# Moving the row normalisations behind the low query half, one value product into slot 4, and half of the probability casts to GpSimd

## What is computed

```
xn = layernorm(ctx, gamma_media, beta_media)
ln = layernorm(layernorm(x), gamma_lat, beta_lat)
q  = ln @ Wq + bq;   k, v = split(concat([xn, ln]) @ Wkv + bkv)
attn = softmax(q k^T * 128**-0.5)            # per head, 256 x 512
x1 = x + concat_heads(attn @ v) @ Wo + bo
```

## Time and profile before

| | |
|---|---|
| median of 3 runs (lowest, highest) | 1898.28 us (1897.49, 1898.93) |
| the profiled execution | 1898.91 us |
| its span | 1896.6 us |
| TensorE busy / VectorE / ScalarE / GpSimd | 95% / 78% / 70% / 21% of the span |

### The profile page before, as it was taken

One profiled execution on the slowest core, in us unless ns is written; L12 is line 12 of the kernel. 1 busy time (PEld: TensorE's weight loads), 2 busy tenths in 40 slices (PEclk: granted clock), 3 DMA queues, 4 the chain that ended last, 5 costly groups with the idle time before them and its releaser, 6 DMA issues.

```text
span 1896.6 us, 39969 instructions
## 1 busy us (share of the span) xinstructions
PE 1804.8 (95%) x12874; PEld 1672.3 (88%) x12874; DVE 1484.5 (78%) x3620; ACT 1330.2 (70%) x2554; POOL 390.1 (21%) x610
## 2 busy tenths in 40 slices
PE   6889999999999999999689999999999999999999
PEld 5778888888888878888578999999999999999998
DVE  6787788788787787777567788888888888888876
ACT  5777787777776777767556777766777777666753
POOL 1222222222222222222244111111111011111100
PEclk9999999999999999999889999999999999999999
DMA  4454565455554444344353933342442323433400
GB/s 143 85 126 106 127 148 123 103 130 138 125 135 82 91 84 93 80 91 79 79 109 111 298 73 73 80 85 57 85 86 64 83 65 74 84 79 63 86 7 12
DMA packets 355420, 182.25 MB, mean 96 GB/s; under 512 B 292512, under 2 KB 340512, under 8 KB 355360
## 3 DMA queue, kind: packets, MB, share of 16 engines
q1 hardware_dynamic: 346656, 146.88, 32.1%
q0 software_dynamic: 8704, 34.61, 10.2%
HBM read 97.29 MB, written 21.23 MB: 62 GB/s over the span
## 4 chain that ended last, share of the span: by engine, by line
PE 80%; DVE 10%; issue 4%; ACT 3%; DMA 1%; POOL 1%; DVEq 0%; SPq 0%; POOLq 0%; ACTq 0%
PE ring L2016 9%; PE ring L2018 9%; PE ring L2017 8%; PE ring L726 8%; PE ring L728 8%; PE ring L727 8%; PE sim L726 3%; PE sim L2018 3%; PE sim L2016 3%; PE sim L2017 3%; PE sim L728 3%; PE sim L727 3%; DVE a_parts L647 2%; PE ps_x L726 2%; PE ps_x L727 2%
## 5 line engine op out<-in xcount | busy, mean ns | idle before, releaser
L2016 PE MATMUL ring<-b_xch,b_wel 128*128 128x256 f32 x1024 | 289.8, 283 | 0.5 <-DVE b_act_e L1639 0.5
L2018 PE MATMUL ring<-b_xcl,b_weh 128*128 128x256 f32 x1024 | 286.4, 280 | 0.0
L2017 PE MATMUL ring<-b_xch,b_weh 128*128 128x256 f32 x1024 | 286.1, 279 | 0.0
L394 POOL TENSOR_SCALAR a_parts<-a_pr,a_rinv 128x512 f16<-128x512 f32 x240 | 170.4, 725 | 413.0 <-DVE a_rinv L638 310.2
L486 ACT ACTIVATE a_pr<-sim,a_nmax 128x512 f32<-128x512 f32 x256 | 173.2, 684 | 40.9 <-DVE a_nmax L627 39.9
L2017 PEld LDWEIGHTS ring<-b_xch,b_weh 128*128 128x128 f32 x1024 | 193.4, 189 | 0.0
L2016 PEld LDWEIGHTS ring<-b_xch,b_wel 128*128 128x128 f32 x1024 | 192.1, 188 | 0.7 <-DVE b_act_e L1639 0.7
L2018 PEld LDWEIGHTS ring<-b_xcl,b_weh 128*128 128x128 f32 x1024 | 192.1, 188 | 0.0
L1355 ACT ACTIVATE b_heh<-b_act_e 128x512 fp32r<-128x512 f32 x128 | 80.7, 630 | 146.7 <-DVE b_act_e L1639 112.8
L627 DVE TENSOR_REDUCE a_nmax<-sim 128x1 f32<-128x512 f32 x256 | 165.8, 682 | 11.3 <-PE sim L728 10.6
L647 DVE SCALAR_TENSOR_TENSOR a_parts<-a_pr,a_rinv,a_parts 128x512 f16<-128x512 f32 x240 | 169.8, 748 | 6.0 <-POOL a_parts L394 6.0
(11 more groups left out here) (362 smaller groups left out, 6350.1 us busy)
## 6 DMA issues: line engine op xcount, KB each, us to landing
b_w2l_raw<-in_W2T POOLq DMA_DIRECT2D x16, 1088.0 KB, 8.7
b_even_b<-rows_between SPq DMA_DIRECT2D x16, 1024.0 KB, 5.6
b_w1l_raw<-in_W1T POOLq DMA_DIRECT2D x16, 1024.0 KB, 8.4
b_w1l_raw<-in_We SPq DMA_DIRECT2D x8, 768.0 KB, 4.6
expert_halves<-b_w1h SPq DMA_DIRECT2D x8, 768.0 KB, 3.4
expert_halves<-b_w1l SPq DMA_DIRECT2D x8, 768.0 KB, 4.9
b_weh<-expert_halves SPq DMA_DIRECT2D x8, 768.0 KB, 8.7
b_wel<-expert_halves SPq DMA_DIRECT2D x8, 768.0 KB, 10.1
```

The source lines that it names most:

```text
L394: nc.gpsimd.tensor_scalar(parts[:, 0, t, :], pr[:, h % 2, t, :], rinv[:, h % 2, t:t + 1], 1.0, ALU.mult, ALU.mult).then_inc(prob_ready, 1)
L2016: nc.tensor.matmul(out, ll, rh, start=(n == 0), stop=False)
L2017: nc.tensor.matmul(out, lh, rh, start=False, stop=False)
L2018: last = nc.tensor.matmul(out, lh, rl, start=False, stop=(n == len(parts) - 1))
```

## The change

- In slots 0 to 3 the statistics and applications of the layer norm stand on VectorE behind the low half of Q (even slots) or of K and the inverses (odd slots), and no longer in front of the low half of K.
- V7 is made in slot 4 between Q3 and O3, and no longer at the end of slot 3.
- The second plane's cast runs on GpSimd as two instructions of 128x512 (`low_cast`), behind `normalise_probs` and behind `rstd_of`, which itself has moved behind `normalise_probs`. It waits for the transpose of plane 1 and for ScalarE's cast of plane 0. ScalarE keeps the cast of plane 0.
- The semaphore `cast` becomes `cast_hi` and `cast_lo`: O waits for both, a DMA transpose for the cast that last read its plane. O of heads 0 and 4 waits for the values explicitly.
- The semaphore `consts` is folded into `pool_step`.

```diff
@@ slot
+        if h == KT:
+            out.append(("V", 2 * KT - 1))
...
-        return out + [("V", v) for v in {0: (4,), 2: (5,), 3: (6, 7), H - 2: (0, 1), H - 1: (2, 3)}.get(h, ())]
+        return out + [("V", v) for v in {0: (4,), 2: (5,), 3: (6,), H - 2: (0, 1), H - 1: (2, 3)}.get(h, ())]
@@ cross
-            for part, made, done in ((0, prob_ready, turned_hi), (1, part_lo, turned_lo)):
+            for part, made, done, cast in ((0, prob_ready, turned_hi, cast_hi), (1, part_lo, turned_lo, cast_lo)):
                 take(made, n * ST + ST)
                 if not (isinstance(b, int) and b == 0 and h == 0):
-                    take(cast, n * 2 - 1 + part)
+                    take(cast, n)
@@ gpsimd
+        def low_cast(b, h):
+
+            n = b * H + h
+            take(turned_lo, n * 16 + 16)
+            take(cast_hi, n + 1)
+            for t in range(ST):
+                last = nc.gpsimd.tensor_scalar(ptl[:].rearrange("p k (t q) -> p t k q", t=ST)[:, t], turned[:, 1, t],
+                                               1.0 / PART_SCALE, 1.0, ALU.mult, ALU.mult)
+            last.then_inc(cast_lo, 1)
+
@@ gpsimd, turn
-                if nxt and h < 3:
-                    rstd_of(b + 1, h)
...
                 elif nxt:
                     normalise_probs(b + 1, 0)
+                if nxt and h < 3:
+                    rstd_of(b + 1, h)
                 if not nxt:
                     other.beside(h, "probs")
+                if nxt:
+                    low_cast(b, h)
@@ scalar, casts
-            for part, there, dst in ((0, turned_hi, pth), (1, turned_lo, ptl)):
-                act.wait_ge(there, n * 16 + 16)
-                nc.scalar.activation(dst[:].rearrange("p k (t q) -> p t k q", t=ST), turned[:, part], ACT.Copy,
-                                     scale=1.0 / PART_SCALE).then_inc(cast, 1)
+            act.wait_ge(turned_hi, n * 16 + 16)
+            nc.scalar.activation(pth[:].rearrange("p k (t q) -> p t k q", t=ST), turned[:, 0], ACT.Copy,
+                                 scale=1.0 / PART_SCALE).then_inc(cast_hi, 1)
@@ vector, turn
-                if nxt:
-
-                    if 1 <= h <= 3:
-                        norm_apply(b + 1, h - 1)
-                    if h < 3:
-                        norm_stats(b + 1, h)
-                else:
+                if not nxt:
                     other.beside(h, "maxima")
...
+                    if j == (1 if h % 2 == 0 else 0) and nxt:
+
+                        if 1 <= h <= 3:
+                            norm_apply(b + 1, h - 1)
+                        if h < 3:
+                            norm_stats(b + 1, h)
@@ tensor, fill
-                    pe.wait_ge(cast, (of_b * H + h) * 2 + 2)
+                    pe.wait_ge(cast_hi, of_b * H + h + 1)
+                    pe.wait_ge(cast_lo, of_b * H + h + 1)
+                    if h % KT == 0:
+                        pe.wait_ge(ring_lo, order.done(("V", KT - 1 + h), i))
```

More of the change, by code:

```diff
@@ L230, in latent_attention @@
     affine_in, c_small, bo_in = sem("affine_in"), sem("c_small"), sem("bo_in")
-    consts = sem("consts")
     w_hi, w_lo, bq_ready = sem("w_hi"), sem("w_lo"), sem("bq_ready")
@@ L240, in latent_attention @@
         sem(n) for n in ("sim_full", "max_ready", "exp_done", "inv_ready", "prob_ready"))
-    part_lo, turned_hi, turned_lo, cast = sem("part_lo"), sem("turned_hi"), sem("turned_lo"), sem("cast")
+    part_lo, turned_hi, turned_lo = sem("part_lo"), sem("turned_hi"), sem("turned_lo")
+    cast_hi, cast_lo = sem("cast_hi"), sem("cast_lo")
     wo_full, res_ready, x1_ready, x1_out = sem("wo_full"), sem("res_ready"), sem("x1_ready"), sem("x1_out")
@@ L376, in gpsimd @@
         nc.gpsimd.affine_select(out=ident[:], in_=ident[:], compare_op=ALU.not_equal, fill=1.0, base=0,
-                                pattern=[[-1, P]], channel_multiplier=1).then_inc(consts, 1)
+                                pattern=[[-1, P]], channel_multiplier=1).then_inc(pool_step, 1)
         def rstd_of(b, k):
@@ L383, in rstd_of @@
                 .then_inc(pool_step, 1)
-            pool.wait_ge(pool_step, b * 3 + k + 3)
+            pool.wait_ge(pool_step, b * 3 + k + 4)
             nc.gpsimd.tensor_tensor(rstd[:, k, :], veps[:, k, :], mhalf[:], ALU.pow).then_inc(rstd_ready, 1)
@@ L804, in project_out @@
                 last.then_inc(wo_full, 1)
-        pe.wait_ge(consts, 1)
+        pe.wait_ge(pool_step, 3)
         transposes(0)
@@ L856, in fill_count @@
         return last.at(at + last.names[at:].index(name)) + 1
-    names = ("consts", "kv_ready", "x1_ready", "x1_out", "ring_full", "ring_lo", "sim_full", "exp_done", "wo_full", "took")
-    sems = dict(zip(names, (consts, kv_ready, x1_ready, x1_out, ring_full, ring_lo, sim_full, exp_done, wo_full, took)))
+    names = ("kv_ready", "x1_ready", "x1_out", "ring_full", "ring_lo", "sim_full", "exp_done", "wo_full", "took")
+    sems = dict(zip(names, (kv_ready, x1_ready, x1_out, ring_full, ring_lo, sim_full, exp_done, wo_full, took)))
     return FirstHalf(sync, gpsimd, scalar, vector, tensor, ident, mhalf, (ring, sim, ps_c, ps_x), sems, fill_count)
```

## The result

The change makes the kernel slower: 1929.26 us (1925.71 to 1932.51, 4 runs) against 1898.26 us, a ratio of 1.0164 with a 95% interval of 1.0151 to 1.0177. The profiled execution is the shortest of the four, 1925.71 us with a span of 1923.9 us, 26.8 us above the one of before. The mean clock granted to TensorE over the four runs is 0.980, 0.977, 0.977 and 0.976, in the order of their times; in the kernel before it was 0.99.

What follows compares the result with a forecast made beforehand. TensorE, 96% busy in the attention, was taken to lose 3.65 us per turn at single waits. Terms +0.6 + 0.1 - 0.7 + 0.9 + 0.4 = +1.3 us, times 15, +19 us, gave 1917.3 us; range 1887 to 1938.

Steps and rivals of the forecast that it cites:

- O waits for the second cast: Slots 3, 5, 7: `ptl` ready 1.55 us after `pth` instead of 0.95, delaying O2, O4, O6; O6 +0.6 us.
- O2 at 1.7 plus 0.4 for collisions: Slot 3: O2 waits 1.7 us for head 2's cast behind `rstd_of`; three VectorE-GpSimd meetings add +0.4 us.
- part 3: Second cast moved to GpSimd, two instructions per head taking 1.36 us; ScalarE's saving of 7.6 us per turn costed at nothing.
- The collision: VectorE's two-input instructions and GpSimd's casts stretch when overlapping: +0.9 us in slot 5, +0.4 in slot 3.
- the blocking rule: Two-SBUF-input VectorE and SBUF-reading GpSimd instructions exclude each other, the later blocked; trace said to agree to 0.1 us.
- Part 1, the wait at S(4): Slot 2: moving 1.83 us of normalisation behind Q2's low half cuts the 1.67 us wait to about 0.05.
- The term of 1.1: Slot 3: some 1.1 us of the 1.6 gained return as S(5)'s wait for K5, whatever GpSimd does.
- Part 2, -0.7: Slot 4: V7 between Q3 and O3 removes S(6)'s 0.71 us wait, -0.7 us per turn.
- Times 15: +19 us: All 15 changed turns lose +1.3 us each, turns without the expert split counted alike: +19 us.
- The casts slip between: Rival: collisions shift but cost nothing on the path, -0.2 to +0.1 us per turn, 1895 to 1901; chance 0.12.
- The cast is dearer: Rival: the GpSimd pair takes 1.9 us, 0.55 more in slots 3, 5 and 7, 1942 us; chance 0.10.
- The faster rival: Rival: cast in time at O6 and O2, within 0.95 us of `pth`; -18 us, 1880 us; chance 0.15.

Runs made afterwards that it cites:

- The divided casts: Changed kernel with plane 1 of heads 2, 4 and 6 cast on ScalarE again, the other five heads on GpSimd; 1895.86 us, ratio 0.9985.
- part 3 alone: Kernel before with plane 1's casts on GpSimd; normalisations, `rstd_of` and V7 as before; 1914.29 us, ratio 1.0080.
- The run with reads that nobody waits for: Kernel before plus two GpSimd instructions per head reading a weight tile and writing scratch, `consts` folded; 1914.52 us, ratio 1.0080.
- the run that only writes: Kernel before plus three GpSimd memsets of a scratch tile per head, result unused; 1904.31 us, ratio 1.0029.
- part 2 alone: Kernel before with only V7 moved to slot 4; 1897.48 us, ratio 0.9992.
- the filled waits: Changed kernel plus unused identity matmuls in front of O2's wait (4) and O4's wait (6) in each turn; 1903.69 us, ratio 1.0029.
- part 1 alone: Changed kernel with V7 back in slot 3 and both casts on ScalarE; 1894.75 us, ratio 0.9974.

## Why the prediction was right, and where it was not

The forecast was slower, 1917.3 us; measured was 1929.3, within the stated range (1887 to 1938) and just inside the forecast's own (1907 to 1930). The direction was right, and so were the waits for the cast and the collisions as its causes, but the total is in part luck: the terms of the sum came out smaller than I had them, and a loss that the sum had no term for filled the gap and more. The lost time is 31 us against 19.

- **O waits for the second cast: right.** O6 +0.6, measured 0.55: the pair took 1.20 us and not 1.36, and O6 started 0.15 us behind it and not 0.05. O2 at 1.7 plus 0.4 for collisions, measured 2.0. The divided casts show that the loss is these three casts. The run with part 3 alone shows that O2 and O4 wait only when the other two parts have freed the scores in front of them, as the walk through the slots has it. That `rstd_of` stands in front of the cast of head 2 is shown by moving it: 1.84 us of idle time fell to 0.16.
- **The collision: right.** Slot 5 lost 2.0 us where I had 1.27 + 0.9; L647's pair went from 1.40 to 1.76. The place was wrong: I expected S(7) to wait over 2 us, and the whole wait stands at O4, with none at S(7). The run with reads that nobody waits for reproduces the mean; of its 16 us loss, some 10 go beyond the run that only writes. I wrote that the rows agree with the blocking rule to 0.1 us. They do to 0.1 and 0.2: at 384.54 the stretch is 0.39 us where 0.52 of the other instruction were left, at 30.21 it is 0.44 of 0.64.
- **Part 1, the wait at S(4): right, with its return in the turns with the split.** I said that 1.1 us would come back at S(5) whatever GpSimd does. With the casts on ScalarE it was 1.22 to 1.86 in turns with the split and nothing in turns 9 to 13, which I had counted alike. The term of 1.1 was mis-sized by a collision that I had priced in part 3 only, that with the normalisation on GpSimd: the layer-norm application took up to 1.40 instead of 0.73 us with no cast on GpSimd at all, and VectorE's chain to K5 started that much later. The wait grows with that stretch from turn to turn (1.22, 1.6, 1.86 us), but no run took the collision away by itself.
- **Part 2, -0.7: wrong by itself.** "The wait goes: -0.7 us" overlooked that V7 pushes O3, and with it the affine and both casts behind O3's high half on ScalarE, against O4. The run of part 2 alone shows 0.95 us there and no gain (ratio 0.9992). In the full change this was covered by the larger wait for GpSimd, so it made no difference to the sum.
- **"Times 15: +19 us": the failing step.** At full clock turns 1 to 13 lost 11.7 us, not 17: the turns without the split lost 0.5 and not 1.3. Up to the first store the kernel gained 4.8 us where the sum had a loss of 1.3. All runs with casts on GpSimd have this (108 to 109.5 us against 112 to 116), so it goes with the cast leaving ScalarE. Part of it is the clock, 0.97 there against 0.94 before; the waits behind it were not traced. And the sum had no term for the clock in the turns. I worked out that O2 and O4 would each wait for about 2 us, and priced each at its own length. The 20.9 us that the slow stretches cost in the profiled run are the largest single item, and the filled waits, which take nothing away but idleness, give 21.3 us back between the profiled executions and 25.6 on the medians.
- **The rivals.** "The casts slip between" falls with L660 at 0.916 and a turn that is 1.1 us longer at full clock. "The cast is dearer" falls with 0.70 us per instruction, the price of the nearest row. The faster rival decided at 0.95 us behind `pth`; the cast was through 1.40 us behind it at the earliest (slot 7).

What stays open: why the clock falls after a 1.84 us wait in turn 4 and not after 1.76 and 1.86 in turn 3, and how much of the medians' extra 4 us over the profiled run is more of the same (the mean clocks of the four runs, 0.980 down to 0.976, speak for it, but only one was profiled in detail).

## What to carry to other kernels

Before an operation is moved to a less busy engine, ask who waits for its end, not how full either engine is: here TensorE was not waiting for ScalarE, and three of eight casts stood with no slack in front of it. Check what the new instruction reads against what the neighbour reads at that moment: with both reading SBUF, the two casts in slot 5 took 1.81 us instead of 1.20, and VectorE's two instructions beside them 1.76 instead of 1.40. A TensorE wait should be priced with what comes after it: in five turns, two pauses of 2 us were followed by another 3 us of lost clock. Matmuls that fill such pauses were close to free here (turns of 61.5 to 62.1 us, at full clock).

## What was not expected of the hardware

The granted clock fell to 1.2 GHz for some 3.4 us in the middle of a stream of matmuls, behind pauses of about 2 us; the kernel before, with waits of up to 1.51 us (by the bracket) in the same turns, never showed it there. Over turns 1 to 13 of all fourteen profiled kernels the clock fell 24 times, each time within 1.6 us of the end of a pause with a bracket of 1.76 us or more. There were 30 such pauses, so six were not followed by a fall. None of the 67 pauses of 1.50 to 1.75 us was. A single pause was enough: in part 1 alone those of 1.76 to 1.79 us did it (turns 4 to 7 at 0.97) and those of 1.75 did not, and with `rstd_of` behind the cast those of 1.86 did it and those of 1.73 to 1.75 did not. What sets the six apart is not settled by these runs.

Two VectorE instructions that meet a two-input GpSimd instruction of 1.29 us stretch from 1.40 to 2.52 us, by nearly the whole of it, while GpSimd's keeps its length. The collision goes unnoticed in busy shares, where it reads as more work.
